# A mixture-of-experts layer on one core: new expert products, a new order ahead of the first product, and earlier routing steps

## The reference

```
x = x + fp8(layernorm(x)) @ fp8(context[batch]) + mask[batch]       # one scale for all x, one for all context
n = layernorm(x)
scores = sigmoid(n @ router_w.T)                                    # 32 experts in 8 groups
idx, w = top 4 experts of a token within its 3 best groups; w normalised, times 2.5
# each expert takes its first C = 160 tokens in token order (its slots)
G, U = Xp @ W_gate[e], Xp @ W_up[e]                                 # 160x1024 by 1024x512
Y    = (silu(G) * U) @ W_down[e]                                    # 160x512 by 512x1024
out[token of slot] += Y * weight of slot
out += silu(n @ shared_gate.T) * (n @ shared_up.T) @ shared_down.T  # inner size 1024
x = x + out
```

## Time and profile before

| | |
|---|---|
| median of 3 runs | 2148.41 us (2147.27 to 2150.02) |
| profiled execution | 2145.67 us, of which the span of instructions is 2144.1 us |
| PE busy | 1950.9 us (91% of the span) |
| DVE busy | 1407.3 us (66%) |
| ACT busy | 971.0 us (45%) |
| POOL busy | 494.2 us (23%) |
| mean granted clock of PE | 0.987 |

### The profile page before, as it was taken

The page is one execution under the profiler, slowest core; times in us unless marked ns, Lnnn a source line. Parts: engine busy times, 40 slices in busy tenths (PEclk is TensorE's granted clock), DMA queues, the critical chain, the costliest instruction groups (busy, mean ns, idle before and its releaser), DMA issues.

```text
span 2144.1 us, 48521 instructions
## 1 busy us (share of the span) xinstructions
PE 1950.9 (91%) x19329; PEld 1610.9 (75%) x19344; DVE 1407.3 (66%) x2536; ACT 971.0 (45%) x1429; POOL 494.2 (23%) x603
## 2 busy tenths in 40 slices
PE   0048999999999999999999999799999999999997
PEld 0026568767766866776786687499999999999996
DVE  5887575567557556655644553388878878878874
ACT  8654222222222222221221121277777877877874
POOL 2100210210112021011102101433334334334332
PEclk9989999999999999999999999899999999999998
DMA  9935312212222221221112014499999999999993
GB/s 381 359 90 167 93 54 70 89 69 62 70 80 60 70 90 50 68 81 69 50 50 79 34 47 158 128 301 326 329 334 323 326 338 319 329 339 320 326 339 71
DMA packets 144405, 371.95 MB, mean 173 GB/s; under 512 B 18128, under 2 KB 18160, under 8 KB 144272
## 3 DMA queue, kind: packets, MB, share of 16 engines
q1 hardware_dynamic: 122352, 311.14, 41.1%
q0 software_dynamic: 20736, 58.81, 12.9%
q10 hardware_dynamic: 1184, 0.15, 0.0%
HBM read 314.76 MB, written 55.35 MB: 173 GB/s over the span
## 4 chain that ended last, share of the span: by engine, by line
PE 78%; DVE 7%; issue 7%; DMA 4%; POOL 2%; SPq 1%; ACT 0%; ACTq 0%; POOLq 0%; DVEq 0%
PE ps L1270 48%; PE ps L1281 10%; PE ps L1464 10%; PE ps L1308 3%; PE ps L1434 2%; DMA W<-in_ctx_in 2%; PE ps L1413 2%; PE ps L1335 1%; PE ps L1353 1%; DMA BIG<-in_ctx_in 1%; DVE st L990 1%; POOL slots L511 1%; DVE X L986 1%; POOL rs L504 1%; DMA X<-in_x 1%
## 5 line engine op out<-in xcount | busy, mean ns | idle before, releaser
L1270 PE MATMUL ps<-XT,W 128*128 128x256 f16 (+1 forms) x12288 | 1121.6, 253 | 9.3 <-DVE W L1208 5.0
L1270 PEld LDWEIGHTS ps<-XT,W 128*128 128x128 f16 x12288 | 1026.5, 98 | 95.4 <-issue 19.4
L1208 DVE SCALAR_TENSOR_TENSOR W<-BIG,W 128x2048 f16<-128x2048 f32 x192 | 435.3, 2292 | 1.5 <-issue 1.4
L787 ACT ACTIVATE W<-BIG 128x2048 f16<-128x2048 f32 x192 | 365.1, 1904 | 0.0
L1281 PE MATMUL ps<-W,HH 128*128 128x512 f16 x1536 | 342.8, 380 | 11.4 <-DVE sc L1110 7.5
L246 POOL TENSOR_TENSOR expo<-expo 128x1 f32<-128x1 f32 x159 | 104.6, 658 | 880.0 <-ACT X L823 374.7
L1281 PEld LDWEIGHTS ps<-W,HH 128*128 128x128 f16 x1536 | 149.6, 98 | 190.1 <-issue 20.2
L729 ACT ACTIVATE SG<-ps 128x256 f32<-128x256 f32 x128 | 49.1, 384 | 475.3 <-PE ps L1270 475.3
L1135 DVE SCALAR_TENSOR_TENSOR SG<-ps,SG 128x256 f32<-128x256 f32 x128 | 54.3, 424 | 269.8 <-ACT SG L729 269.8
L1464 PE MATMUL ps<-HH,W 128*128 128x160 f16 x3072 | 217.9, 233 | 0.0
L1464 PEld LDWEIGHTS ps<-HH,W 128*128 128x128 f16 x3072 | 213.4, 98 | 0.2 <-DVE HH L1237 0.2
(11 more groups left out here) (167 smaller groups left out, 1900.7 us busy)
## 6 DMA issues: line engine op xcount, KB each, us to landing
BIG<-in_w_gate SPq DMA_DIRECT2D x64, 1024.0 KB, 10.1
BIG<-in_w_up SPq DMA_DIRECT2D x64, 1024.0 KB
BIG<-in_w_down SPq DMA_DIRECT2D x64, 1024.0 KB
X<-in_x SPq DMA_DIRECT2D x16, 1024.0 KB, 5.1
X<-in_mask POOLq DMA_DIRECT2D x16, 1024.0 KB, 8.3
xn_rows<-FR SPq DMA_DIRECT2D x32, 512.0 KB
out_rows<-X SPq DMA_DIRECT2D x32, 512.0 KB
W<-in_x SPq DMA_DIRECT2D x6, 2048.0 KB, 19.3
```

The lines of the kernel that those rows point to most:

```text
L787: ac.activation(dst, stage, ACT.Copy, scale=W_SCALE).then_inc(x_hi, 1)
L1208: ve.scalar_tensor_tensor(out=lo[cut], in0=src, scalar=W_SCALE, in1=hi[cut], op0=ALU.mult, op1=ALU.subtract).then_inc(x_lo, 1)
L1270: ins = te.matmul(out_ps, a[:, k, cols], b[:, k, :], start=n == 0, stop=n == len(steps) - 1)
```

## The change

- Experts, down: the activations become stationary. For the first 128 slots 24 products of 512 columns give rows directly; the last 32 slots are done as four products side by side (`TC` = 32, `TQ` = 4, `TD` = 256), each with weights of 32 columns, 256 columns of the output, and 32 partitions of its own. No transposes back, no second copy.
- Experts, tokens: gathered as 128 full rows and 32 rows in quarters (a quarter row of 256 numbers in each of 128 partitions), likewise for the adding to the output. 10 transposes of 128 rows instead of 16 of 80. Slot table, indices and slot weights are laid out to match (five loads, seven index operations).
- Expert weights are laid out so that a partition's 8 KB of a piece lie together in DRAM.
- `LOADS`, `PEAKS`: x ahead of context; x's maximum and scale are made first, after x's last peak, and context's after b3; x's rounding comes ahead of context's.
- First group's residual: statistics and shift of the two tiles interleaved. First group: context tile 9 rounded after the third down block, the last weight splits ahead of the slots, `xn_stores(1)` ahead of the context loads on SP.
- Logits: high half to partitions 0 to 63, low half to 64 to 127; `lg` and `sel` have 128 partitions, and the selection sums four blocks.
- PE's second down block waits for `d_pos`, signalled by the first instruction of `route_slots`, instead of `d_route`.
- Last group: picks in step 2, positions after step 3 on PE, slots in step 4.

```diff
-        logit_ps = PS[2][0:2 * E, 0:G]
+        et_tail = PS[6][:, 0:KD * TC]
+        dn_tail = PS[7][:, 0:TD]
+        logit_ps = PS[2][:, 0:G]
...
-        PEAKS = [("b", 0), ("x", 0), ("b", 1), ("x", 1), ("c", 0), ("x", 2), ("c", 1), ("x", 3), ("c", 2), ("x", 4),
-                 ("c", 3), ("x", 5), ("c", 4), ("x", 6), ("c", 5), ("b", 2), ("b", 3), ("x", 7)]
+        PEAKS = [("b", 0), ("x", 0), ("x", 1), ("b", 1), ("x", 2), ("c", 0), ("x", 3), ("c", 1), ("x", 4), ("c", 2),
+                 ("x", 5), ("c", 3), ("x", 6), ("c", 4), ("c", 5), ("x", 7), ("b", 2), ("b", 3)]
...
+                src = rows((w_gate, w_up, w_down)[m // 2], (e * 2 + m % 2) * P, P)
+                sp.dma_start(ew_stage[m], src).then_inc(ld_ew[m], 16)
...
-                sp.dma_start(tab[:, :, :], slot_dram.rearrange("(c p) w -> p c w", p=HC)).then_inc(ld_tab, 16)
+                slots = slot_dram.rearrange("(e s) w -> s e w", e=E)
+                sp.dma_start(tab[:, :, 0, :], slots[0:P]).then_inc(ld_tab, 16)
+                for c in range(TQ):
+                    sp.dma_start(tab[c * TC:(c + 1) * TC, :, 1, :], slots[P:C]).then_inc(ld_tab, 16)
...
             pool.wait_ge(amax_ready, 1)
-            gp.partition_all_reduce(sc1[:, 5:6], sc1[:, 4:5], P, bass.bass_isa.ReduceOp.max).then_inc(amax_all, 1)
-            pool.wait_ge(amax_ready, 2)
             ch.link(gp.partition_all_reduce(sc1[:, 1:2], sc1[:, 0:1], P, bass.bass_isa.ReduceOp.max))
             gp.tensor_tensor(sc1[:, 1:2], sc1[:, 1:2], root[:, :], ALU.pow).then_inc(amax_all, 1)
+            pool.wait_ge(amax_ready, 2)
+            gp.partition_all_reduce(sc1[:, 5:6], sc1[:, 4:5], P, bass.bass_isa.ReduceOp.max).then_inc(amax_all, 1)
...
+                for dst, src, u in ((xg[b], xn_dram, 0), (xgt[b], xn_quarters, 1)):
+                    gp.indirect_dma_start(out=dst, out_offset=None, in_=src[:, :],
...
             act.wait_ge(scales_ready, 1)
-            ctx0_scaled(0)
-            ctx0_scaled(1)
-            act.wait_ge(scales_ready, 2)
             x_scaled(0, 0)
...
+            act.wait_ge(scales_ready, 2)
+            ctx0_scaled(0)
+            ctx0_scaled(1)
+            xq_evac(0)
             ctx0_scaled(2)
             ctx0_scaled(3)
-            xq_evac(0)
...
+                act.wait_ge(x_dn, e * 3 + (u + 1))
+                dst = ybuf[b][:, u * HALF:(u + 1) * HALF] if u < 2 else ytail[b]
+                ac.activation(dst, PS[4 + u][:, :] if u < 2 else dn_tail, ACT.Copy,
+                              scale=wts[:, bass.ds(e * 3 + u, 1)]).then_inc(x_y, 1)
...
+                if piece == ("b", 2):
+                    fp8_scale(0)
...
+            x0_round(0)
+            fp8_scale(1)
+            ve.tensor_tensor(sc1[:, 9:10], sc1[:, 3:4], sc1[:, 7:8], ALU.mult).then_inc(scales_ready, 1)
+            x0_round(1)
+            for m in range(4):
+                ctx0_round(m, tiles=1 if m == 3 else 2)
...
-                ch.link(ve.tensor_tensor(e_pr[:, :, :, :], e_eq[:, :, :, :],
-                                         pos_ps.unsqueeze(2).to_broadcast([P, NT, TOPK, E]), ALU.mult))
+                ve.tensor_tensor(e_pr[:, :, :, :], e_eq[:, :, :, :],
+                                 pos_ps.unsqueeze(2).to_broadcast([P, NT, TOPK, E]), ALU.mult).then_inc(d_pos, 1)
...
-                                ins = te.matmul(logit_ps, rw[:, k, :], xT[v][:, k, :], start=k + v == 0,
-                                                stop=k == KD - 1 and v == 1)
+                                ins = te.matmul(logit_ps[2 * E * v:2 * E * (v + 1), :], rw[:, k, :], xT[v][:, k, :],
+                                                start=k == 0, stop=k == KD - 1)
...
-                    if ic == (KS - 1 if front else 5):
+                    if ic == (KS - 1 if front else 3):
...
-                        pe.wait_ge(d_route, g + 1)
+                        pe.wait_ge(d_pos, g + 1)
...
+                passes = ((hhi, whi), (hhi, wlo), (hlo, whi))
+                for h, ks in ((0, range(KI - 1)), (1, range(KI - 1)), (0, (KI - 1,)), (1, (KI - 1,))):
...
+                            ins = te.matmul(PS[4 + h][:, :], a[:, k, 0:P], w[:, k, h * HALF:(h + 1) * HALF],
+                                            start=k == 0 and n == 0, stop=k == KI - 1 and n == 2)
+                for k in range(KI):
+                    for n, (a, w) in enumerate(passes):
+                        for c in range(TQ):
+                            ins = te.matmul(dn_tail[c * TC:(c + 1) * TC, :], a[:, k, P:C], w[:, k, c * TD:(c + 1) * TD],
+                                            start=k == 0 and n == 0, stop=k == KI - 1 and n == 2)
```

More of the change, by code:

```diff
@@ L460, in _ @@
                                    pattern=[[1, P]], channel_multiplier=-1))
-            for half in range(2):
+            for half in range(4):
                 ch.link(gp.affine_select(out=sel[:, :], in_=sel[:, :], compare_op=ALU.not_equal, fill=1.0,
@@ L832, in expert @@
                     if ic == 0:
-                        wait(act, x_dn, e * 4)
+                        wait(act, x_dn, e * 3)
                     ac.activation(ehT[0][:, ic, :], h32[ic % 2][:, 0:C], ACT.Copy).then_inc(x_hh, 1)
-                    if ic == 0 and before:
-                        for u in (2, 3):
-                            rows_out(e - 1, 1 - b, u)
                     if more and ic < 3:
@@ L853, in expert @@
                     ew_hi(e + 1, 1 - b, 5)
-                else:
-                    for u in (2, 3):
-                        rows_out(e, b, u)
-            expert(0, 0, before=False)
+            expert(0, 0)
             expert(1, 1)
@@ L976, in split_lo, with add_cross @@
                                         op1=ALU.subtract).then_inc(sw_lo, 1)
+            def add_cross(f, b, j):
+                dve.wait_ge(p_xm, 16 * f + 16)
+                for h in range(2):
+                    at = xbuf[b][:, j, h * HALF:(h + 1) * HALF]
+                    dve.wait_ge(pe_xa, 4 * f + 2 * j + h + 1)
+                    bank = PS[4 + h] if j and isinstance(f, int) and f == 0 else PS[2 + h]
+                    ve.scalar_tensor_tensor(out=at, in0=bank[:, :], scalar=sc1[:, 9:10], in1=at,
+                                            op0=ALU.mult, op1=ALU.add).then_inc(d_x2, 1)
@@ new lines, in ln2_stats, with shift @@
+            def ln2_stats(f, b, j):
+                dve.wait_ge(d_x2, 4 * f + 2 * j + 2)
+                for h in range(2):
+                    ch.do(ve.bn_stats(st2[:, j, h, :], xbuf[b][:, j, h * HALF:(h + 1) * HALF]))
+                ch.sync()
+                carry(ve, 1)
+                ch.link(ve.bn_aggr(mv2[:, j, :], st2[:, j, :, :]))
+                ve.tensor_scalar(ve2[:, j:j + 1], mv2[:, j, 1:2], LN_EPS, None, ALU.add).then_inc(d_var, 1)
+            def shift(f, j):
+                dve.wait_ge(p_rs, 2 * f + j + 1)
+                ve.scalar_tensor_tensor(out=nb2[:, j:j + 1], in0=mv2[:, j, 0:1], scalar=-1.0, in1=rs2[:, j:j + 1],
+                                        op0=ALU.mult, op1=ALU.mult).then_inc(d_nb, 1)
@@ L1010, in _ @@
             split_lo(0)
-            residual(0, 0)
-            shift(0)
+            add_cross(0, 0, 0)
+            ln2_stats(0, 0, 0)
+            add_cross(0, 0, 1)
+            shift(0, 0)
+            ln2_stats(0, 0, 1)
+            shift(0, 1)
             split_lo(1)
@@ L1148, in group @@
                         x_round(g + 1, ic - first - 3, M_main)
-                    if ctx and ic - first == 6:
+                    if ctx and ic == 6 and not first:
                         ctx_round(g, 2 * g + 9, 1, 2 * g + 10)
-                    if ic == 6 and not front:
+                    if ic == 4 and not front:
                         route_slots(g)
@@ L1157, in group @@
                     residual(g + 1, 1 - r)
-                    shift(g + 1)
-                    route_slots(g)
+                    for j in range(NT):
+                        shift(g + 1, j)
                 if first:
@@ L1423, in _, with expert @@
             pe.wait_ge(d_out, 4 * GROUPS)
[L1425 to L1438 removed]
+            def expert(e, b, more=True):
                 pe.wait_ge(x_lo, e * 6 + 4)
@@ L1445, in expert @@
                     product(PS[ic % 2][:, G:G + C], EW[b][1], eT, KD, cols).then_inc(x_gu, 1)
-                    if ic == 0 and before:
-                        rows_transpose(e - 1, 1, after=e)
-                wait(pe, x_y, e * 4)
                 if more:
@@ L1490, with pieces @@
     T, D = 4096, 1024
+    def pieces(w):
+        e, rows, cols = w.shape
+        return w.reshape(e, 2, rows // 256, 128, cols).transpose(0, 1, 3, 2, 4).reshape(e * 256, rows // 256 * cols)
     data = {
```

290 lines of the change are left out of this document (121 added, 169 removed).

## The result

The changed kernel takes **2078.2 us** (median of 4 runs, 2077.95 to 2081.25), the kernel before 2148.0: a ratio of 0.9677 (95% interval 0.9660 to 0.9694), 69.8 us less. The forecast was 2090 with a range of 2070 to 2113. In the first series of the experiments the two took 2073.7 and 2143.3 us (0.9675, 0.9658 to 0.9691). The profiled execution is the one of 2081.25 us; its span is 2079.6 us, 64.5 less than before.

The account below looks back on a forecast made before the run. PE held 91% of the span, with DVE's chain becoming the experts' bound. Terms -21 -2.4 -15 -7 -6 +2.5 -9 = -58 from 2145.67 gave 2087.8; the median lies 2.7 higher: 2090 us, range 2070 to 2113.

Parts of the forecast that it names:

- Experts: Experts: without row transposes DVE's chain becomes the bound, period 22.45 us, 0.68 saved in each of 31 periods, -21 us.
- The free length of strips: Experts' down products: the strips may take up to 2.9 us at no cost, since DVE's chain bounds the period.
- The rule weighed there: Experts' strips: loads overlap products only with different row groups or the spare buffer; three strips measured 2.38 times faster.
- Strips in turn: Rival, experts and logits: strips run one after another, 5.3 us, and logits save nothing; 2187 us, chance 0.12.
- Logits: Each group's logits: 8 pairs on two column groups run together, 0.9 instead of 1.87 us; -15 us over 16 groups.
- Position bank: Groups: the stall before the second down product goes, 0.5 us in each of 14 groups, -7 us.
- Group 0: First group: PE's 2.75 us residual wait goes and the 3.88 us wait shrinks; -6 us, bounds -4 and -8.
- x ahead of context: Start, before the first product: x's scale made first; net +2.5 us, bounds -1 and +7.
- this wait: Start: POOL's 6.92 us after its maximum over partitions, taken as a change of its code, before x's scale at 102.4.
- Last group two steps ahead: Last group to first expert: slots start 10.5 us earlier, PE's first expert start moves -9 us, bounds -4 and -12.
- End: After the last down product: three copies, two under the strips, replace 16 transposes and four row copies; -2.4 us.
- DMA takes over: Rival, experts: DMA share already 1.04, no faster period possible, the -21 us gone; 2111 us, chance 0.1.

Follow-up runs that it names:

- The undoing: Changed kernel with PE's second down product waiting again for the whole slot routing instead of the one read of the position bank: 2087.4 us.
- weight wait in parts: Changed kernel with an expert's first gate product waiting only for the two gate pieces, the up products for their own pieces: 2033.9 us.
- loads held: Changed kernel with the shared weights' loads held back until x's scale is ready: 2071.2 us.
- old order: Changed kernel with the start's loads, peaks, all-reduces, scalings and roundings ordered as in the kernel before: 2066.4 us.
- old weight rows: Changed kernel with expert weights back in memory rows of 2 and 4 KB instead of 8 KB: 2076.2 us.
- the strips in turn: Changed kernel with each column strip's 12 products done before the next strip, and the two logit column groups one after the other: 2125.2 us.
- both gains: Changed kernel with PE's wait for split weights cut in parts and the start in its order from the kernel before: 2028.7 us.

## Why the prediction was right, and where its steps were off

The bound among the experts, which carries the largest term, was right in mechanism and in size. That the sum came within 12 us is in part luck: by the table, three stages took 9.5 us more than forecast (3.9 of them in one execution's group 15) and four took 15.8 us less, and these misses partly cancel.

*Experts* (-21, measured -22.5). The steps held: PE's work 21.05 forecast and 21.15 measured, period 22.45 and 22.47, the idle time 1.4 and 1.33, its releaser, the clock at 1.00. The 1.5 us more lie mostly in the first expert, which takes 22.1 us for 23.5. The bound was read from a trace in which it only just showed; the row that says so is PE's own:

```profile
1736.13 3.49 PE L1270 MATMUL ps<-XT,W 128*128 128x160 f16 x48 [0.19 <-DVE W L1208]
```

PE waited so for a weight split 25 times, 5.0 us in all. The 0.44 us of the prediction's sum is the idle time of the weight loads (PEld), not PE's. On the chips of the experiments both kernels' periods are shorter (22.97 us with the old experts, 22.25 and 22.32 in turn with the new) and as far apart. The lower end taken for the strips was the right one: they take 1.42 us. The 0.2 us added there for the change of shape is twice what its rows give, since 16 logit products in 1.87 us are 0.11 us over 16 x 0.11, for both sides together. The free length of strips, 2.9 us, comes out at 4.09 - 1.45 = 2.6.

*The rule weighed there.* The Trainium skill ("TensorE: Matmul & The Clock Gate", The mechanism) ties the overlap of loads to a different row group or the spare buffer. Here strips with the same rows ran four at once, 48 loads and products in 1.42 us, so the trace doesn't bear out the reading that made it a rival. Against single products of 109 ns the gain is 3.7, for four strips; that page of the Trainium skill has 2.38 for three.

*Strips in turn* (2187). The mechanism exists, since the order of the loop alone decides between the cases, but its price was too high: 5.3 us per expert took no account of the seams, and 4.09 us make a period of 23.74, not 25.05. Even in turn the changed kernel is faster than before, by 18 us (0.8%).

*Logits* (-0.95 each, measured -0.87), the mechanism right. *Not seen*: the selection behind them. With four row blocks its weights became 128 rows high, as all around it, and the distance over its products fell from 0.56 to 0.37 us; it was called "the same columns" and priced at nothing. With 0.1 at the boundary ahead of it: 16 x 0.3 = 5 us. That the height is the cause wasn't tested by itself.

*Position bank* (-0.5, measured -0.7). The stall was read from the trace; what a stop costs besides wasn't: a row of 24 down products is 5.34 us long, but without a stop the next begins 5.18 us after it. The undoing shows 0.69.

*Group 0* (-6 and 1 for the logits). The residual's wait went and the one at 228.43 shrank from 3.88 to 2.05 us. The stage takes 89.8 us in the two profiles of the changed kernel, 4.5 less than before, and 87.1 to 87.4 in three edits that leave it alone (weight wait in parts, loads held, old order), 7 less; with the old weight rows it takes 88.0. Part of the difference is the 24 products behind that wait, in part at half speed (7.02 us), in the first profile, and in the second a wait of 3.73 us for DVE after the fourth column (1.3 to 2.3 elsewhere) with the 144 products behind it in 17.26 us for 15.89. What makes that wait longer stays open.

*x ahead of context* (+2.5, measured +5.6, inside the bounds). The failed step is "this wait": 6.92 us for POOL's code, read where nothing was being loaded. In the new order 4 MB of shared weights are in flight, and it takes 10.67 us in that profile. The DMA share, the last number but one, tells the two apart (windows view, the kernel before and the changed one):

```profile
103.70:110.50 6.80, 0.00 (x0) 0.00 (x0) 4.38 (x2) 1.67 (x1) 0.00 (x0) 1.00 0.00 0
...
94.20:104.80 10.60, 0.00 (x0) 0.00 (x0) 1.67 (x1) 0.00 (x0) 0.00 (x0) 1.00 1.01 359
```

The 6 us taken for the change back were right (5.78). x's scale came at 105.5 for 102.4, and the roundings ended at 142.7 for 139.3.

*Last group two steps ahead* (-9, bounds -4 and -12; measured -14.1). The sum given for it, -10.5 + 5.7 - (0 to 5), ends at -9.8, so the bound of -12 had no term behind it. The failed step is the constant length of the slot writes. Their long ones stood beside DVE's weight splits and the move takes them out from under. The start in the group and the table (7.1 us for 9.0) were priced rightly or dear.

*End* (-2.4, measured -5.7). The copies give 2.4 as said. From POOL's last step to the end of the span 11.0 us pass for 14.3 before: the last adding transfer carries 32 rows in quarters of 1 KB in place of 80 full rows. That was not priced; no run takes it apart.

*DMA takes over* (0.10): no; share 0.96 in the period, and 1.02 in the one of 21.08 us, at 358 GB/s, with no wait for a load from the third expert on.

## To carry over

Where a chain of another engine is only just hidden behind PE, price it ahead of PE's savings: the saving ends where the chain begins, and here one wait cut in parts gave 40 us more, over half as much as the whole change. Products on narrow column strips want to alternate; the same products strip by strip take nearly three times as long here. A duration read from one place holds only with the neighbours it had there: an indirect write beside a long DVE operation, or a change of POOL's code beside a large load, is another number.

## What the hardware showed beyond expectation

- *POOL beside DVE's long operations.* The copy of two index columns takes 175 ns in the kernel before and 2275 ns in the changed one (28 of them each), now that it stands beside a weight split. The profile counts it as busy time, not as a wait. Timeline of the changed kernel, POOL and then DVE:

```profile
1649.41 2.35 POOL L566 COPY gix<-gidx 128x2 uint32 x1
...
1649.33 2.28 DVE L1218 SCALAR_TENSOR_TENSOR W<-BIG,W 128x2048 f16<-128x2048 f32 x1
```

 The two end within 0.15 us of each other, and in the traces of the changed kernel, the strips in turn, the weight wait in parts and both gains no short copy lies inside a split: POOL gets no copy done until the split is over. What they share isn't shown by these runs.
- *PE starts some four products of a new strip beside the last of the old one*, by the pairs of starts at each seam of the strips in turn.
- *The gap that I read as a change of POOL's code* depends on its direction as well. Behind an all-reduce it is 6.7 to 7.6 us with a DMA share of 0.00 beside it, and 10.3 to 10.7 us with 0.71 to 1.02. Ahead of one it is 5.8 to 6.1 us whatever the queues do: 5.78 us with a share of 0.06 in the changed kernel, and 6.11 us with 1.05 in the kernel before (windows):

```profile
90.00:96.00 6.00, 0.00 (x0) 0.00 (x0) 4.14 (x3) 0.00 (x0) 0.04 (x1) 1.00 1.05 389
```

- *The granted clock after the same idle time differs between executions.* In group 0 a wait of 2.05 us is followed by 24 products in 5.35 us in one profile and in 7.02 in another of the same kernel.
